# A fused two-layer AdaLN transformer: the local output product taken per half of a sequence from split operands, and two sets of weights loaded a phase sooner

## The reference, cut to what matters

```python
# block 1: linear attention with learned feature maps, then a plain MLP (128 -> 512 -> 128)
# block 2: six layers of: local windowed attention, then a gated MLP
for i in range(6):
    x = attn_layer(shift_tokens(x), Wqkv[i], q_scale[i], k_scale[i], Wo[i]) + x
    x = ffn_layer(shift_tokens(x), ln_g[i], ln_b[i], W1[i], b1[i], W2[i], b2[i]) + x
# block 3: multi-query attention; block 4: a plain MLP (128 -> 512 -> 128)
def attn_layer(x, Wqkv, qs, ksc, Wo):          # 16 heads of 64, windows of 32 queries and 64 keys
    q, k, v = split(x @ Wqkv)                  # 128 -> 3 * 1024
    q, k = rotary(l2norm(q) * qs), rotary(l2norm(k) * ksc)
    out = local_attention(q, k, v)             # softmax over the 64 keys of a window
    return out @ Wo                            # 1024 -> 128
```

## Time and profile before

| | |
|---|---|
| three runs | 3886.91, 3890.16, 3891.97 us (median 3890.16) |
| profiled execution | 3886.54 us, of which 3884.5 us from the first to the last instruction |
| granted TensorE clock, mean over the span | 0.975 |
| PE, PEld busy | 3664.8 and 2936.8 us |
| DVE, ACT, POOL busy | 3139.0, 2885.5 and 2454.0 us |
| local layers, share of the span | about 3040 of 3884 us |

### The profile page before, as it was taken

How to read it: one execution, slowest core, us unless ns; L and a number is a source line. 1 busy time by engine, 2 the same in 40 slices (tenths; PEclk the granted TensorE clock), 3 DMA queues, 4 the chain that set the end, 5 groups by cost and what they waited for, 6 DMA issues and landing times. The chain is left out here.

```text
span 3884.5 us, 189323 instructions
## 1 busy us (share of the span) xinstructions
PE 3664.8 (94%) x70910; PEld 2936.8 (76%) x70910; DVE 3139.0 (81%) x9411; ACT 2885.5 (74%) x8517; POOL 2454.0 (63%) x2552
## 2 busy tenths in 40 slices
PE   6769999999999999999999999999999999899997
PEld 3458888678887788876888868888688886466665
DVE  5778888788887788877888878888788887666667
ACT  4658888578886688875888848888488885677775
POOL 2647777477774677755777647777377772455553
PEclk8879999999999999999999999999999999899997
DMA  1013333233333233332333323333233331100000
GB/s 42 6 38 84 81 81 82 62 81 81 81 80 79 64 82 81 81 88 52 82 82 81 82 60 81 80 82 82 60 85 81 81 82 43 35 1 0 0 0 28
DMA packets 305289, 245.99 MB, mean 63 GB/s; under 512 B 74485, under 2 KB 299860, under 8 KB 304340
## 3 DMA queue, kind: packets, MB, share of 16 engines
q1 hardware_dynamic: 305108, 243.72, 24.8%
HBM read 24.54 MB, written 2.12 MB: 7 GB/s over the span
## 5 line engine op out<-in xcount | busy, mean ns | idle before, releaser
L1220 POOL TENSOR_TENSOR wa_t<-wa_t,wa_rn 128x512 f32<-128x512 f32 x768 | 786.4, 1045 | 280.3 <-DVE wa_rn L1048 277.4
L880 ACT ACTIVATE wa_pb<-wa_sc,wa_nm 128x64 f32<-128x64 f32 x3072 | 672.6, 330 | 365.4 <-DVE wa_nm L1070 337.9
L1226 POOL TENSOR_TENSOR wa_t<-wa_t 128x512 f32<-128x512 f32 x384 | 496.9, 1294 | 402.5 <-DVE wa_t L1024 402.2
L1022 DVE TENSOR_TENSOR wa_t<-wa_pj,wa_ctab 128x512 f32<-128x512 f32 x768 | 528.1, 688 | 206.0 <-PE wa_ta L624 136.2
L45 PE MATMUL wa_pj<-lw_wqkv_high,wa_xhigh 128*128 128x512 f32 x1152 | 531.9, 462 | 36.1 <-DVE wa_t L1024 17.9
L863 ACT ACTIVATE wa_sq<-wa_pj 128x512 f32<-128x512 f32 x768 | 486.4, 635 | 60.2 <-PE wa_pj L47 57.9
L1235 POOL TENSOR_TENSOR wa_t<-wa_t 128x512 f32<-128x512 f32 x384 | 490.9, 1278 | 0.0
L47 PE MATMUL wa_pj<-lw_wqkv_high,wa_xlow 128*128 128x512 f32 x1152 | 459.5, 399 | 0.0
L46 PE MATMUL wa_pj<-lw_wqkv_low,wa_xhigh 128*128 128x512 f32 x1152 | 456.9, 397 | 1.3 <-issue 1.3
L1030 DVE TENSOR_REDUCE wa_raw<-wa_sq 128x16 f32<-128x1024 f32 x384 | 449.4, 1170 | 0.0
L683 PE MATMUL wa_ob<-wa_oT,lw_wo 128*128 128x128 f32 x3120 | 418.1, 277 | 2.9 <-DVE wa_on L1082 2.7
(11 more groups left out here) (287 smaller groups left out, 8626.8 us busy)
## 6 DMA issues: line engine op xcount, KB each, us to landing
wa_vv<-wa_vt SPq DMA_DIRECT2D x2304, 65.0 KB
wa_vv<-wa_vt SPq DMA_DIRECT2D x1152, 32.5 KB
lw_wqkv<-L_ffn_Wqkv SPq DMA_DIRECT2D x6, 1536.0 KB, 6.2
lw_xs<-yT SPq DMA_DIRECT2D x96, 64.0 KB
lw_fs<-yT SPq DMA_DIRECT2D x48, 128.0 KB
lw_xs<-yT SPq DMA_DIRECT2D x96, 63.8 KB
lw_fs<-yT SPq DMA_DIRECT2D x96, 63.8 KB
lw_wo<-L_ffn_Wo SPq DMA_DIRECT2D x6, 512.0 KB, 4.2
```

The lines of the kernel that those rows point to most:

```text
L880: last = nc.scalar.activation(pb[:, u.par(2), p, e, :], SC[:, e, p * KEYS:(p + 1) * KEYS], ACT.Exp, bias=nm[:, u.par(2), e, p:p + 1])
L1022: nc.vector.tensor_tensor(t1[:, b, j], x, table(ctab, slice(0, HD)), ALU.mult)
L1220: nc.gpsimd.tensor_tensor(here, here, rn[:, u.par(1), j * HG:(j + 1) * HG].unsqueeze(2).broadcast_to((128, HG, HD)), ALU.mult).then_inc(s. ...
L1226: nc.gpsimd.tensor_tensor(t1[:, b, 0], t1[:, b, 0], t2[:, b, 0], ALU.add).then_inc(s.qadd_done, 1)
```

## The change

**The output product.** `oT` and `Wo` are kept as two float32r parts each. ACT copies the transposed result twice: in full float32 to `oF` (which lies in the gated MLP's `hid`) and rounded to the high part. POOL subtracts the two for the low part, between its scalings and its addition for the keys. PE makes the product once for a half of the heads of a whole sequence (both tiles, 256 columns), in three passes over four weight blocks: 12 matmuls. It does so in the slots k = 1 and k = 3 alone (`closes`), and in k = 4 of the drain, behind the transposes of the exponentials, no longer ahead of them. The result lies in the upper half of the bank SC0 (in the drain partly in OB0), so the scores of that slot wait until DVE has added it. DVE adds 256 columns, in the same slots.

**`Wo`** of the first layer is split by POOL in the norm ahead (two steps more), that of each next layer in the gated MLP's last but one group, each as two operations over 128 by 1024 elements. POOL also takes the drain's slots 1 to 3.

**The loads.** The 22 transfers of the linear attention are issued by SP in the norm ahead, after the input transfers of groups 2 to 7 (two, then four after each). The seven of the first plain MLP are issued at the start of the linear attention, those of the second at the start of the norm ahead of it. POOL splits all MLP weights there, one operation per group, in groups 1 to 4; DVE's and POOL's splits within `plain_mlp` go.

```diff
@@ PE, front
-                    if u.has(5):
-                        h = u.half(5)
-                        pe.wait_ge(s.oT_out, u.count(1, 5, 2))
-                        if u.has(4):
-                            pe.wait_ge(s.norm_done, u.count(1, 4, 1))
-                        else:
-                            pe.wait_ge(s.wo_out, u.count(1, 6, 3))
-                        for j in range(PR):
-                            last = nc.tensor.matmul(OB[:, 0, Y0:Y0 + 128], wo[:, PR * h + j, :], oT[:, u.tile(5), PR * h + j, :],
-                                                    start=(j == 0), stop=(j == PR - 1), skip_group_check=True)
-                        last.then_inc(s.wo_done, 1)
                     if u.has(3):
...
                         transposes(TB, lambda p: pb[:, u.par(3), p].rearrange("q e k -> q (e k)")).then_inc(s.pT_done, 1)
+                    lag = u.closes()
+                    if lag:
+                        h = u.half(lag)
+                        pe.wait_ge(s.oT_low, u.count(1, lag, 2))
+                        pe.wait_ge(s.wo_out, u.layer * (2 * NB) + (u.product() + 2))
+                        if u.tail and u.k == 3:
+                            pe.wait_ge(s.norm_done, u.count(1, 4, 2))
+                        for j in range(PR):
+                            last = three_passes(nc, output(u), [x[:, PR * h + j, :] for x in wo], [x[:, h, j, :] for x in oT],
+                                                start=(j == 0), stop=(j == PR - 1), skip_group_check=True)
+                        last.then_inc(s.wo_done, 1)
@@ PE, back, ahead of the mask and the scores
+                        if u.closes():
+                            pe.wait_ge(s.wo_out, u.layer * (2 * NB) + (u.product() + 3))
@@ which slots close a half
+    def closes(self):
+        if self.k == UPS:
+            return 5
+        lag = {1: 6, 3: 5}.get(self.k)
+        return lag if lag and self.has(lag) else 0
@@ where the product lies
+        def output(u):
+            return OB[:, 0, (u.k - 3) * SEQ:(u.k - 2) * SEQ] if u.tail and u.k >= 3 else SC[:, 0, PR * KEYS:PR * KEYS + SEQ]
@@ ACT
                         act.wait_ge(s.oT_done, u.count(1, 4, 1))
-                        if u.was(8):
-                            act.wait_ge(s.wo_done, u.product(8))
-                        nc.scalar.activation(oT[:, u.tile(4), PR * u.half(4):PR * (u.half(4) + 1), :],
+                        nc.scalar.activation(oF[u.par(4)], TA[:, :], ACT.Copy)
+                        nc.scalar.activation(oT[0][:, u.half(4), :, u.tile(4) * 128:(u.tile(4) + 1) * 128],
@@ DVE, between rotate(u, 0) and rotate(u, 1)
-                    if u.has(5):
-                        dve.wait_ge(s.wo_done, u.product(5))
...
+                    lag = u.closes()
+                    if lag:
+                        dve.wait_ge(s.wo_done, u.layer * (2 * NB + 1) + (u.product() + 2))
...
+                        nc.vector.tensor_tensor(yT[:, col], output(u), yT[:, col], ALU.add).then_inc(s.wo_out, 1)
@@ POOL, after normalise(1) and normalise(0)
+                    if u.has(4):
+                        here = u.half(4), slice(None), slice(u.tile(4) * 128, (u.tile(4) + 1) * 128)
+                        pool.wait_ge(s.oT_out, u.count(1, 4, 2))
+                        nc.gpsimd.tensor_tensor(oT[1][(slice(None), *here)], oF[u.par(4)].rearrange("p (a b) -> p a b", a=PR),
+                                                oT[0][(slice(None), *here)].bitcast(F32), ALU.subtract).then_inc(s.oT_low, 1)
@@ POOL, gated MLP of the layer ahead
+                    if u.at == NGRP - 2 and not u.final:
+                        split_output(u)
@@ PE, whole
-                    pe.wait_ge(s.w_o, layer * 16 + 16)
+                    pe.wait_ge(s.wo_low, layer + 1)
@@ LinearWeights, issued from the norm ahead
+    def load(self, sp, n):
+        for dst, src in self.pairs[max(4 * n - 10, 0):max(4 * n - 6, 0)]:
+            sp.dma_start(dst, src).then_inc(self.loaded, 16)
@@ NetworkWeights
+    def split(self, pool, n, out_done):
+        if n == 1:
+            pool.wait_ge(self.loaded, 16 * (3 + MCH))
+            nc.gpsimd.tensor_tensor(self.w1p[0][:, :], self.w1[:, :], self.zero.broadcast_to((128, MLP)), ALU.add).then_inc(self.w1_split, 1)
...
@@ main
-        layernorm_modulate(nc, "n0_", g, g.yT, mod(0, 1), mod(0, 0), from_dram=a["L0_attn_x"])
+                layernorm_modulate(nc, "n0_", g, g.yT, mod(0, 1), mod(0, 0), from_dram=a["L0_attn_x"], load=linear.load)
+                linear_attention(nc, g, w, linear, network)
...
-        layernorm_modulate(nc, "n3_", g, g.yT, mod(1, 4), mod(1, 3))
+            layernorm_modulate(nc, "n3_", g, g.yT, mod(1, 4), mod(1, 3), load=network.load, split=network.split)
```

More of the change, by code:

```diff
@@ L39, in glu_rows, with three_passes @@
     return min(GW, GLU - j * GW)
[L42 to L47, removed]
+def three_passes(nc, out, lhs, rhs, start=True, stop=True, **more):
+    nc.tensor.matmul(out, lhs[0], rhs[0], start=start, stop=False, **more)
+    nc.tensor.matmul(out, lhs[0], rhs[1], start=False, stop=False, **more)
+    return nc.tensor.matmul(out, lhs[1], rhs[0], start=False, stop=stop, **more)
 def phase_semaphores(nc, ctx, tag, more=()):
@@ L373, in has, with product @@
         return self.was(lag) and (not self.tail or self.k < lag)
-    def product(self, lag):
-        here = self.layer * (UPL + 1) + (UPS * self.lead + self.k - lag + 2)
-        return here if self.loop is None else here + self.loop * UPS
+    def closes(self):
[3 more added lines that the diff above has]
+        return lag if lag and self.has(lag) else 0
+    def product(self):
+        last = 2 * NB - 1 if self.k == UPS else 2 * self.lead - (2 if self.k == 3 else 3)
+        return last if self.loop is None else last + self.loop * 2
     def count(self, per, lag, r):
@@ L521, in local_layers @@
         on = sb("on", [128, 2, PR, 2, HD])
-        oT = sb("oT", [128, 2, HEADS // 2, 128])
+        oT = [sb("oT_" + n, [128, 2, PR, SEQ], F32R) for n in ("high", "low")]
         st = gb("st", [128, TPG, 6])
@@ L534, in local_layers @@
         SC, OB = ps("sc", 2), ps("ob", 2)
+        oF = [hid[:, n, :] for n in range(2)]
         NA, NX, Y = PJ[1], PJ[0], TA
@@ L833, in whole @@
                     pe.wait_ge(s.xn_parts, first.n(1, 1))
+                    pe.wait_ge(s.wo_out, layer * (2 * NB) + 2 * NB)
                     chunk(first, 0)
@@ L991, in _ @@
                 nc.vector.memset(kT[:, :, :, 0:WIN], 0.0)
-                nc.vector.memset(oT[:, 1, PR:2 * PR, :], 0.0).then_inc(s.wo_out, 2)
-                nc.vector.memset(vt[:, :, :, :, HD:VW], 1.0)
+                for part in oT:
+                    nc.vector.memset(part[:, 1, :, :].bitcast(F32), 0.0).then_inc(s.wo_out, 1)
+                nc.vector.memset(vt[:, :, :, :, HD:VW], 1.0).then_inc(s.norm_done, 1)
                 nc.vector.memset(raw[:, :, 1], 1e-24)
@@ L1280, in whole @@
                     turn(LayerGroup(layer, 0))
+                    slot(Slot(layer, 1, NB))
+                    slot(Slot(layer, 2, NB))
                     turn(LayerGroup(layer, 1))
+                    slot(Slot(layer, 3, NB))
                     turn(LayerGroup(layer, 2))
                     groups(pool, layer, multiply, closing, turn)
+                pool.sem_inc(s.oT_low, 1)
                 split_input(0, 32, 1)
@@ L1384, in _ @@
             def _(sp):
[L1385 to L1394 removed]
+                later.load(sp, 0)
             ALL_LOADED = 16 * 22
```

188 lines of the change are left out of this document (111 added, 77 removed).

## The result

The changed kernel takes 4104.57 us (median of four runs, 4103.12 to 4107.29) against 3889.09 us for the kernel before (four runs beside it): a ratio of 1.0554, 95% interval 1.0537 to 1.057. It is slower by 215.5 us. The forecast was 4110 us with a range of 4040 to 4175.

The account below looks back on a forecast made before the run. PE's list and the loops through PE and DVE were taken to bound it within 0.2 us. Slots +227, `Wo`'s split +6 and +4, loads -6 and -9 make +222 us: 4110 us, range 4040 to 4175.

Parts of the forecast that it names:

- What bounds the kernel: Local attention slots: PE's list and two loops, through PE and DVE, within 0.2 us; old product fills PE's wait for TB.
- loop one: Local slot, through PE: exponentials, keys' eviction from TB, transposes, value projection, scores, next exponentials; 6.45 us without slack.
- PE's missing 0.89 buys 0.07: Slots without a product: dropping PE's 0.89 us product shortens the slot only from 6.57 to 6.5 us.
- The product in the open: Slots k = 1, 3: the product, 1.33 us behind the transposes, delays DVE's addition; slot of 7.91 us.
- DVE is last: Slots with a product: DVE's steps end at 4.39 us after the keys' eviction, PE's scores at 4.26.
- The cover of ACT's copy and POOL's subtraction: Local slots: ACT's 0.5 us copy and POOL's 1.27 us subtraction lie in idle time and cost nothing.
- `Wo`'s split: POOL's split between layers and in the norm ahead of layer one: +6 us and +4 us.
- The loads: Sooner weight transfers: -6 us at the first projection (-3 to -13), -9 us in the MLPs.
- only PE waits: Rival: in slots with a product DVE's addition isn't last; 7.75 us a slot, 4083 us in all; chance 0.17.
- PE's list counts: Rival: PE's list bounds the slots, each pair gains 0.45 us; faster, 3804 us; chance 0.12.
- unhidden loads: Rival: the product's weight loads aren't hidden at 256 columns, 1.33 us more a pair; 4349 us; chance 0.05.
- the cancellation: Rival: gain and waits cancel as the two kinds of slots lend each other time, within 8 us of before; chance 0.03.

Follow-up runs that it names:

- run 7: The kernel before with one of the four matmuls of each output product, three quarters left out: 3890.67 us, ratio 1.0004.
- run 4: The changed kernel with DVE's addition of the product moved behind the rotation of the keys: 4094.08 us, ratio 1.0522.
- run 6: The changed kernel with each output product made twice, same result: 4387.89 us, ratio 1.129.
- run 8: The changed kernel without ACT's full copy and POOL's subtraction, the second pass reading the high part again: 4094.73 us, ratio 1.0529.
- run 10: The changed kernel with the product ahead of the exponentials' transposes, without ACT's full copy and POOL's subtraction: 3979.22 us, ratio 1.0245.
- the early product: The changed kernel with PE making the product ahead of the exponentials' transposes in the closing slots: 4041.11 us, ratio 1.0389.
- run 1: The kernel before with the sooner loads alone, local layers as they were: 3869.30 us, ratio 0.995.
- run 3: The changed kernel with only the product moved ahead of the exponentials' transposes in the closing slots: 4041.11 us, ratio 1.0389.

## Why the prediction was right

**What bounds the kernel** held. A PE that was busy for 98% of the stage had nothing to give, because what its list saved came back as a wait for TB: 0.55 to 0.57 us a slot where 0.62 was worked out from the earlier trace rows, and run 7 shows it with nothing else changed. What the prediction did not have is the wait behind it, that of the value projection for DVE's rotation of the queries. Its loop one counts 0.1 + 0.80 = 0.90 from the free bank to that projection; in the change it is 1.04 over all rounds in the slots without a product, 0.06 to 0.09 behind the end of the rotation (2102.67 + 0.41 = 2103.08, projection at 2103.14). So loop one is some 0.14 longer than its 6.45, and "PE's missing 0.89 buys 0.07" did not come true: these slots take 6.63, where a slot before took 6.60.

**The product in the open** held in each of its terms but one. The transposes start 0.05 to 0.1 after the bank is free (2108.05 + 0.66 = 2108.71, transposes at 2108.76), the product 0.42 later as forecast (0.43). It takes 1.50 us until the next transposes, not 1.33: records stand 0.119 apart, not 0.111, and the first takes 0.20. That is the mis-sized term, by 0.17. It was made up on DVE: the addition starts at 2111.00, 2.29 after the free bank (2.1 forecast), and from there to the maximum it is 2.12 (2113.12 - 2111.00), where 0.33 + 1.26 + 0.70 = 2.29 were added up. The sum, 4.41, stands for 4.39 in the forecast. "DVE is last" is a matter of 0.24: PE's last scores are there at 2112.88, and the maximum starts at 2113.12. Run 4 bears it out: without it a closing slot is 0.14 shorter, and the time 10.5 us.

**The slots:** over all rounds the closing slots take 7.84 for 7.91 and the others 6.63 for 6.5, a pair 14.47 for 14.41. A pair before took 13.20 over all rounds and not the 13.15 of the stretch in the earlier trace rows, so the loss is 1.27 a pair for 1.26. That precision is luck in three places: the two kinds of slots are off by 0.07 and 0.13 in opposite directions, inside the closing slot two terms are off by 0.17 in opposite directions, and the mean before was 0.05 a pair short. The loops' +228 us for +227 rest on that; the mechanism of the closing slot, and the range, do not.

**The weight loads are hidden.** One of the three groups of a product's weight loads in the changed kernel (that of the drains, where the product lies in OB0):

```profile
L46 PEld LDWEIGHTS wa_ob<-wa_oT_low,lw_wo_high 128*128 128x128 f32 x48 | 9.0, 188 | 0.0
```

One takes 188 ns (191 in the loops), and the twelve matmuls follow 119 ns apart although weights are loaded for each; run 6, with twice the matmuls and loads, adds no more than 12 x 0.119 a product. The Trainium skill, "TensorE: Matmul & The Clock Gate", "Part 3: Packing small matmuls", would have these loads in the open, since all of them use every row. The trace doesn't agree, at 256 columns any more than at 512.

**The cover of ACT's copy and POOL's subtraction** was costed at nothing, and in the loops that is what it costs (run 8: 28.91 us a round without them, 28.93 with them). The prediction named the condition on which the cover would go, shorter slots. Run 10 shows what it means: with the early product the same two operations cost 0.57 us a round, 51 us in the loops.

**`Wo`'s split:** the two operations take 1.89 and 2.34 us in the norm ahead, and the phase ends 3.0 later (forecast 4). The local layers lose 231.4 us for the 233 forecast; the rounds have 228 of them, so that some 3 are left for the five boundaries and the drains, where 6 was forecast.

**The loads** were the poorest step. The first projection starts at 44.20, 12.9 earlier, where -6 was forecast and -13 named as the far end. The step that failed is "an input issue takes 13.81 / 8 = 1.73 us". The trace of the kernel before says otherwise when it is asked for the line alone, count, then shortest, median and longest in ns:

```profile
L170 SPq DMA_DIRECT2D n_src<-L_attn_x x8: 368/384/507, 19.8 to 33.2; - x8
```

The 13.81 us were mostly waiting, and for a free input buffer: SP waits (`ring_wait` on `normed` and `turned`) until the group four back has been used, and there are four buffers. The first four issues are 0.45 to 0.54 apart, the fifth is at 26.60, just after DVE has normalised the first group (26.57), and the next ones follow every 2.20 us with DVE's pace. In the trace of the change the last input is issued from 33.63 to 34.01, where the eight together ended at 19.76 + 13.81 = 33.57: 18 other issues fit into the waits at a cost of 0.44. The plain MLPs: PE starts 1.41 us after the start of POOL's low part for 5.92 before, so 4.5 are gained at the first (4.7 forecast); of the 4.7 at the second, 2.4 are left at the end of the kernel. All loads together give 22.1 us (run 1), for 15.

**Against the rivals:** "only PE waits" would have been 4083 us and is 22 off, but the two differ by 0.13 us a closing slot, and run 4 alone tells them apart. "PE's list counts" falls by run 7, "unhidden loads" by the 0.119 us spacing, and the cancellation by the sum.

## What to carry to other kernels

Before work is moved or merged, look at the wait that would stand where it is now. Three quarters of a step of 0.89 us on a 94% busy engine can be free, if the step fills a wait for a bank (run 7), and one product of 1.43 us in the place of two such steps, 0.4 us further on, can cost all of its length (run 6). Follow the engine's list past that wait to the next one: what the first gives back, the second may keep. Where a loop is closed by three engines within 0.2 us of each other, taking work from one of them, or moving it out of the way, gives little or nothing (runs 7 and 4). And a row that stands for several transfers on a queue may be mostly waiting for buffers: before it is divided by the count, look at the single issues.

## What the runs showed that was not expected

- The cost of covered work depends on the slots around it: one copy on ACT and one subtraction on POOL in each slot cost nothing in the loops with the late product (0.02 us a round) and 51 us with the early one (0.57 a round), although the slots of the latter are shorter by only 0.2 us on average (28.10 / 4 for 28.93 / 4).
- The same mask, 64 score and 64 value matmuls take 1.52 to 1.54 us in the closing slots of the change, of run 3 and of run 10 (2111.91 to 2113.45 in the change), and in the slots without a product 1.66 and 1.72 in the change, 1.67 in run 10 and 1.81 and 1.84 in run 3. So it goes by the slot first and by the kernel second. No wait stands in the rows between, and no run here tells the cause.
- A round of the kernel before isn't four equal slots either: in the run of the loads alone, whose loop is the same, they take 6.74, 6.57, 6.45 and 6.55 us by turns, so a mean over 30 slots was the right thing to add up from, and one slot's timeline would have been off by up to 0.17. The slot whose handovers the prediction reads is such a one: from one start of the exponentials to the next it is 2011.14 - 2004.46 = 6.68 us.
